# Pair one-hots of a group by one broadcast comparison, with the weights put on the place rows by GpSimd

## The chip, the cores and the metric

One core of a Trainium2 chip runs the whole program. The metric is the device time of one execution in microseconds (us). The kernel before took 2555.01 us in the median of three runs (2551.72 to 2556.26).

## What is computed

The reference is a graph network on 3125 nodes with 128 features and 103125 edges (`src`, `dst`, sorted by `dst`, and a type from 0 to 3 for each edge):

```python
deg = max(segment_sum(ones, dst), 1);  d = deg ** -0.5
h = relu(layernorm(x)); feat = h
for i in range(10):                                    # hops
    agg = segment_sum(feat[src] * (d[dst] * d[src])[:, None], dst)
    feat = (0.9 * agg + 0.1 * h) * reg[i] + (1 - reg[i]) * feat
x = x + feat
e = relu(layernorm(x))
for _ in range(4):                                     # gated steps
    m = (e @ W_msg.T + b_msg).reshape(n, 4, 128)
    e = gru_cell(segment_sum(m[src, edge_type], dst), e, ...)
return x + e
```

## The kernel before

The kernel never gathers rows. It first counts, for every pair of nodes, the edges between them, by type, as small digits packed in bytes (`big1`), and then does every segment sum as products with these counts. The stages are: setup (0 to 63 us of the profiled execution), counting (63 to 521 us), degrees and factors (to 559 us), ten hops (L691, L706), and four gated steps (L787 and others). The change is in the counting stage.

**The counting stage.** The nodes are cut into 125 groups of 25 targets (`Q = 125`). The edges lie in 825 chunks of 125, one edge per partition and one chunk per column of the tables `keys` (target and source folded into one number), `tab[:, 0]` (the place of the source, 0 to 124) and `tab[:, 1]` (the weight: a power of two that says type and lane). As the edges are sorted by target, a group's edges lie in a window of at most `W = 8` columns, but for rare extra ones (one in this data, L975 to L980 and L612).

For group `q` the engines do this:

- GpSimd (`stage`, L361 to L366): reads the window's first column, waits until the one-hots of two groups earlier have been made (`s_hot`), subtracts the group's offset from 8 keys into `win` (L364), and copies 8 weights (L365) and 8 places (L366). It signals `s_wst`.
- VectorE (`onehots`, L959 to L968): waits for `s_wst` and for TensorE to have used the buffer (`s_hot_used`). One comparison makes the place one-hots of all 8 columns, 128 x 8 16-bit elements (L964). Then 8 operations of 228 elements (`KP`) make the pair one-hots, one per column (L967): equal to the key, times the weight. Each signals `s_hot`.
- TensorE (`count`, L600 to L606): waits for a free bank (`s_taken`) and, before each of its 8 products, for that column's one-hots. Stationary operand: the 125 x 128 place one-hots of a column, read at a step of 8 elements (16 bytes). Moving operand: 228 pair columns. The 8 products add up in one of 8 banks of PSUM.
- ScalarE (`evacuate`, L456 to L461): writes the 228 sums as integers into `words`. After every 8 groups (a block) `part_lanes` (L463 to L472) parts the bytes into `packed` in three operations, and SyncE stores the block to DRAM (16 stores, L309).
- VectorE (`sum_digits`, L983 to L995): once per block, six operations on `packed` that sum the four types' digits into `big1`.

VectorE's order is written out by hand: 4 groups ahead, then blocks of 8 groups with a digit sum behind each, two blocks to an iteration of a loop of 7, then the rest; the last digit sum comes after the stage. One-hots are double buffered. The constants that the comparisons read (`iota_pair`, 228 elements, L346, and `iota_place`, 128 x 8, L348) are made by GpSimd in the setup; VectorE first waits for the constants at L910. Behind the stage TensorE sums the degrees (L647).

A second way through the kernel (`over_any > 0`, the "general" functions) is for inputs whose counts overflow the digits. It does not run here.

```python
def stage(n, q, b, hot, staged):
    pool.wait_ge(hot, W * n + W)
    pool.tensor_tensor(win[0:CH, b, 0, :], keys[0:CH, ds(lo, W)], ..., ALU.subtract)
    pool.tensor_copy(win[0:CH, b, 1, :], tab[0:CH, 1, ds(lo, W)])
    pool.tensor_copy(win_p[0:CH, b, :], tab[0:CH, 0, ds(lo, W)]).then_inc(staged, 1)
```

Of the kernel before, what the change touches and what calls it, by code (L numbers as in the profile page):

```python
# [51 lines left out]
KQ = 1024  # L52
# [5 lines left out]
BANKS = 8  # L58

# [22 lines left out]
def build(nc, x, src, dst, edge_type, layer_reg, w_msg, b_msg, w_ih, w_hh, b_ih, b_hh, out):  # L82
# [7 lines left out]
    with ctx:  # L90
# [68 lines left out]
        with ExitStack() as b:  # L159
            keys = sb("keys", [128, PAD], F32, b)  # L160
            tab = sb("tab", [128, 2, PAD], F16, b)
            win = sb("win", [128, 2, 2, W], F32, b)
            win_p = sb("win_p", [128, 2, W], F16, b)
            win_x = sb("win_x", [128, 3], F32, b)
            hot_pair = sb("hot_pair", [128, 2, W, KP], F16, b)
# [3 lines left out]
            iota_pair = sb("iota_pair", [128, KP], F16, b)  # L169
# [24 lines left out]
        with ExitStack() as b:  # L194
            words = sb("words", [128, 2, KP, BQ], I32, b)
            packed = sb("packed", [128, 2, BLOCK_BYTES], U8, b)
            dig = sb("dig", [128, 3, BLOCK_BYTES // 4], I32, b)
# [58 lines left out]
        s_wst, s_hot, s_hot_used = sem("window_staged"), sem("onehots_made"), sem("onehots_used")  # L256
# [80 lines left out]
        def _(pool):  # L337
# [8 lines left out]
            pool.iota(iota_pair[:, :], [[1, KP]], base=0, channel_multiplier=0,  # L346
# [35 lines left out]
            with pool.If(over_any > 0):  # L382
                pool.wait_ge(s_tables, 1)
                pool.iota(iota_pair_g[:, :], [[1, CA + 1]], base=0, channel_multiplier=0,
                          allow_small_or_imprecise_dtypes=True).then_inc(s_iota_g, 1)
                with pool.Fori(0, LOADS) as load:
# [26 lines left out]
        def _(act):  # L413
# [43 lines left out]
            def evacuate(blk, b, j):  # L457
                q = BQ * blk + j
                act.wait_ge(s_hot_used, W * q + 3 * W)
                summed(q, extras, s_more_used)  # L460
                act.activation(words[:, b, :, j], ps[:, j, 0:KP], ACT.Copy, scale=float(ONE)).then_inc(s_taken, 1)  # L461

            def part_lanes(blk, turn, b, last):  # L463
                act.wait_ge(s_taken, last + 1 + BANKS)
                act.wait_ge(s_digits, blk + 1)
                act.wait_ge(s_packed[b], 16 * turn + 16)
                lanes = words[:, b, :, :].bitcast(U8).rearrange("p n (q l) -> p (n q) l", l=4)
                for l in range(LANES):
                    n = min(LANE, TILES - l * LANE) * TILES * BQ
                    at = l * LANE * TILES * BQ  # L470
                    ins = act.activation(packed[:, b, at:at + n], lanes[:, 0:n, l], ACT.Copy)
                ins.then_inc(s_bytes, 1)  # L472

            def block_of(turn, b, n):
                blk = 2 * turn + b
                act.wait_ge(s_bytes, blk + 1)
                for j in range(n):
                    evacuate(blk, b, j)
                part_lanes(blk, turn, b, BQ * blk + n - 1)

            with act.Fori(0, NB // 2 - 1) as i:
                block_of(i, 0, BQ)
                block_of(i, 1, BQ)
            block_of(NB // 2 - 1, 0, BQ)
            block_of(NB // 2 - 1, 1, Q - (NB - 1) * BQ)
# [79 lines left out]
        def _(pe):  # L565
# [31 lines left out]
            pe.sem_inc(s_hot_used, 2 * W)  # L597
# [40 lines left out]
            with pe.Fori(0, NB - 1) as i:  # L638
                for j in range(BQ):
                    count(BQ * i + j, j % 2, j)  # L640
            for j in range(Q - (NB - 1) * BQ):
                count(BQ * (NB - 1) + j, j % 2, j)
# [194 lines left out]
        def _(dve):  # L837
# [30 lines left out]
            dve.memset(keys[:, :], -1e6)  # L868
# [73 lines left out]
            dve.sem_inc(s_hot, 2 * W)  # L942
# [16 lines left out]
            def onehots(q, b):  # L959
# [3 lines left out]
                dve.wait_ge(s_hot_used, W * q + W)  # L963
                TT(hot_place[0:CH, b, :, :], iota_place[0:CH, :, :],  # L964
                   win_p[0:CH, b:b + 1, :].broadcast_to([CH, 128, W]), ALU.is_equal)
                for w in range(W):
                    TS(hot_pair[0:CH, b, w, :], iota_pair[0:CH, :], win[0:CH, b, 0, w:w + 1],  # L967
                       win[0:CH, b, 1, w:w + 1], ALU.is_equal, ALU.mult).then_inc(s_hot, 1)  # L968
                with dve.If(many > 0):
                    lo = dve.value_load(windows[0:1, ds(q, 1)], min_val=0, max_val=NCH - 1)  # L970
                    with dve.Fori(0, many) as j:
# [8 lines left out]
                        TS(hot_pair_x[0:CH, :], iota_pair[0:CH, :], win_x[0:CH, 0:1], win_x[0:CH, 2:3],  # L980
                           ALU.is_equal, ALU.mult).then_inc(s_more, 1)

            def sum_digits(blk, b):  # L983

                dve.wait_ge(s_bytes, blk + 3)
                x, low, high, lower = packed[:, b, :].bitcast(I32), dig[:, 0, :], dig[:, 1, :], dig[:, 2, :]
                u16 = [d.bitcast(DT.uint16) for d in (low, high, lower)]
# [49 lines left out]
            for j in range(BQ):  # L1037
                onehots(BQ * (NB - 2) + HEAD + j, j % 2)
            sum_digits(NB - 2, 0)
            for q in range(BQ * (NB - 1) + HEAD, Q):  # L1040
                onehots(q, q % 2)
# [55 lines left out]
            with dve.If(over_any > 0):  # L1097
# [6 lines left out]
                step_g(TS(tab_e[width, 1, :], tab_e[width, 0, :], 3, None, ALU.logical_shift_right))  # L1104
                step_g(STT(out=keys[width, :], in0=tab_e[width, 1, :], scalar=float(LANE * TILES), in1=keys[width, :],
# [12 lines left out]
                dve.wait_ge(s_iota_g, 1)  # L1118
# [353 lines left out]
```

## Time and profile before

| | |
|---|---|
| median of three runs | 2555.01 us (2551.72 to 2556.26) |
| the profiled execution | 2550.86 us |
| its span | 2549.3 us |
| TensorE clock granted over the span | 0.921 of full |
| busy over the span: PE, PEld, DVE, ACT, POOL | 2190.8, 1440.7, 1488.7, 335.0, 134.9 us |
| counting stage | 63.01 to 521.21 us |

Engines in the rows: PE is a TensorE product, PEld the load of its stationary operand, DVE is VectorE, ACT is ScalarE, POOL is GpSimd, SP is SyncE. A name with q is the engine's sequencer. L605 is line 605 of the kernel. The clock column gives the granted TensorE clock as a share of 2.4 GHz. A group of instructions shows its busy time, the mean duration of one, and the time in which the engine stood idle just before them with what ended it. Durations overlap where a next instruction starts before the one in front has fully ended, so paces are read from starts. GpSimd's spans are rough.

### The profile page before, as it was taken

The page shows a single profiled execution, that of the slowest core. Times are in us where ns is not written, and L with a number is a line of the kernel's source. Part 1 is how long each engine was busy: PE and PEld are TensorE (multiplying, and loading weights), DVE is VectorE, ACT ScalarE, POOL GpSimd, SP SyncE. Part 2 cuts the span into 40 slices and gives each one's busy share as a digit, 9 for nine tenths or more (in the row PEclk, how much of TensorE's full clock was granted, in tenths as well). Part 3 has the DMA queues.
Part 4 walks back from the last instruction along what each step waited for, and adds up shares of the span by engine and source line. Part 5 has one row for each costly group of instructions (what it writes and reads, how often), then busy time and mean ns, then how long its engine had stood idle before and what let it go on. Part 6 is the DMA issues. An engine that isn't in the chain of part 4 may idle for free.

```text
span 2549.3 us, 41289 instructions
## 1 busy us (share of the span) xinstructions
PE 2190.8 (86%) x14375; PEld 1440.7 (57%) x14886; DVE 1488.7 (58%) x3473; ACT 335.0 (13%) x494; POOL 134.9 (5%) x391
## 2 busy tenths in 40 slices
PE   1544545559999999999799999999999999999996
PEld 1322333348999898988644455444554446544464
DVE  6988999977777777777662234522444324442243
ACT  0322223330000000000121011210112100220000
POOL 1322222200000000000000000000000000000000
PEclk9996555559999999999899999999999999999998
DMA  2000000010000000001400000000000000000001
GB/s 72 21 21 21 21 21 21 28 41 2 1 2 2 2 2 2 1 2 49 139 1 1 1 1 1 1 1 1 1 1 1 1 1 1 1 1 1 1 1 50
DMA packets 22188, 34.32 MB, mean 13 GB/s; under 512 B 2450, under 2 KB 18442, under 8 KB 21469
## 3 DMA queue, kind: packets, MB, share of 16 engines
q1 hardware_dynamic: 19025, 30.56, 3.5%
q8 instruction: 127, 2.08, 0.3%
q10 hardware_dynamic: 2944, 0.93, 0.2%
q14 instruction: 92, 0.75, 0.1%
HBM read 18.04 MB, written 13.45 MB: 12 GB/s over the span
## 4 chain that ended last, share of the span: by engine, by line
PE 75%; DVE 15%; issue 5%; DVEq 2%; DMA 2%; ACT 0%; POOLq 0%; ACTq 0%; POOL 0%
PE ps L787 41%; PE ps L706 26%; DVE hot_pair L967 8%; PE ps L739 3%; PE ps L727 2%; DVEq L961 2%; DVE dig L990 1%; DVE hot_place L964 1%; DVE big L993 1%; DMA big<-in_L_gnn_w_hh 1%; PE ps L647 1%; DMA x_after_hops<-x 1%; PE ps L691 1%; PE ps L605 1%; DVE dig L992 1%
## 5 line engine op out<-in xcount | busy, mean ns | idle before, releaser
L787 PE MATMUL ps<-slots,m_parts 125*128 125x500 fp8e4 (+1 forms) x5600 | 1088.0, 354 | 6.6 <-DVE m_parts L1337 5.2
L787 PEld LDWEIGHTS ps<-slots,m_parts 125*128 125x128 f16 x5600 | 547.4, 98 | 495.7 <-issue 10.0
L706 PE MATMUL ps<-parts,big 125*128 125x256 f16 x6125 | 669.6, 273 | 6.8 <-issue 4.2
L706 PEld LDWEIGHTS ps<-parts,big 125*128 125x128 fp8e4 x6125 | 591.3, 98 | 63.6
L605 PE MATMUL ps<-hot_pair,hot_place 125*128 125x228 f16 x1000 | 230.6, 400 | 256.5 <-DVE hot_pair L967 256.5
L1255 DVE TENSOR_SCALAR slots<-big 128x3200 int32<-128x3200 int32 (+1 forms) x112 | 244.1, 2183 | 279.8 <-PE ps L787 279.7
L605 PEld LDWEIGHTS ps<-hot_pair,hot_place 125*128 125x128 f16 x1000 | 143.1, 149 | 343.8 <-DVE hot_pair L967 283.1
L967 DVE TENSOR_SCALAR hot_pair<-iota_pair,win 125x228 f16<-125x228 f16 x1000 | 262.5, 334 | 3.1 <-issue 3.1
L1357 DVE SCALAR_TENSOR_TENSOR r_parts<-ps,over,r_parts 128x500 f16<-128x500 f32 (+1 forms) x28 | 19.1, 684 | 230.1 <-ACT r_parts L527 230.1
L1364 DVE SCALAR_TENSOR_TENSOR gate_r<-ps,over,gate_r 128x500 f32<-128x500 f32 (+1 forms) x28 | 19.1, 682 | 229.3 <-PE ps L739 221.8
L1183 DVE SCALAR_TENSOR_TENSOR hop_tmp<-ps,coef,g 125x128 f32<-125x128 f32 x250 | 87.6, 350 | 97.9 <-PE ps L706 94.4
L461 ACT ACTIVATE words<-ps 128x228 int32<-128x228 f32 x125 | 72.0, 602 | 354.4 <-PE ps L605 352.2
L964 DVE TENSOR_TENSOR hot_place<-iota_place,win_p 125x1024 f16<-125x1024 f16 x125 | 85.5, 684 | 48.2 <-issue 32.1
L727 PE MATMUL ps<-w_parts,emb_parts 128*125 128x512 f16 x300 | 84.7, 397 | 17.7 <-DVE m_full L1343 9.3
L527 ACT ACTIVATE r_parts<-ps,over 128x500 f16<-128x500 f32 (+1 forms) x28 | 17.7, 634 | 618.6 <-PE ps L787 618.6
L427 ACT ACTIVATE rs<-rs 125x25 f32<-125x25 f32 x3 | 0.7, 224 | 708.7 <-DVE rs L852 708.7
L1185 DVE SCALAR_TENSOR_TENSOR hop_tmp<-ps,coef,hop_tmp 125x128 f32<-125x128 f32 x250 | 87.8, 351 | 8.9
L1164 DVE TENSOR_SCALAR parts<-hop_tmp,scale 125x128 f16<-125x128 f32 x225 | 64.3, 286 | 36.4 <-DVE hop_tmp L1185 33.0
L1178 DVE SCALAR_TENSOR_TENSOR g<-hd,anchor,hop_tmp 125x128 f32<-125x128 f32 x225 | 79.0, 351 | 9.4 <-DVE hop_tmp L1177 0.7
L1167 DVE SCALAR_TENSOR_TENSOR parts<-hop_tmp,scale,parts 125x128 f16<-125x128 f32 x225 | 79.1, 352 | 8.0
L364 POOL TENSOR_TENSOR win<-keys,q_off 125x8 f32 (+1 forms) x125 | 65.3, 523 | 332.7 <-DVE hot_pair L967 318.5
L1343 DVE SCALAR_TENSOR_TENSOR m_full<-ps,bias_msg 125x512 f32<-125x512 f32 x100 | 68.3, 689 | 24.6 <-PE ps L727 23.6
(200 smaller groups left out, 1130.2 us busy)
## 6 DMA issues: line engine op xcount, KB each, us to landing
packed_counts<-packed SPq DMA_DIRECT2D x16, 625.0 KB, 3.3
big<-packed_counts SPq DMA_DIRECT2D x4, 1600.0 KB, 7.3
big<-packed_counts SPq DMA_DIRECT2D x3, 1200.0 KB, 6.5
hd<-in_x SPq DMA_DIRECT2D x1, 1562.5 KB
x_again<-in_x SPq DMA_DIRECT2D x1, 1562.5 KB
x_after_hops<-x SPq DMA_DIRECT2D x1, 1562.5 KB
big<-x_after_hops SPq DMA_DIRECT2D x1, 1562.5 KB
out<-big SPq DMA_DIRECT2D x4, 250.0 KB
```

The lines of the kernel that those rows point to most:

```text
L605: pe.matmul(ps[:, j, 0:KP], hot_place[0:CH, b, :, w], hot_pair[0:CH, b, w, :], start=w == 0, stop=w == W - 1, skip_group_check=True).then_ ...
L706: last = pe.matmul(ps[:, n % RING, 0:2 * F], tot_f8[0:Q, c, a, :], both((parts0, parts1)[par], a), start=a == 0, stop=a == TILES - 1)
L727: last = pe.matmul(ps[0:Q, 6 + a % 2, :], emb_parts[:, h, a, :], w_parts[:, w, :], start=n == 0, stop=n == 2)
L739: last = pe.matmul(out, g_parts[:, w, j * F:(j + 1) * F], value(h), start=start and m == 0, stop=stop and m == 2)
L787: last = pe.matmul(ps[:, k % 2, 0:SIZES[k] * Q], m_parts[0:Q, a, h, t * F:(t + 1) * F], slots_f8[0:Q, t % 2, 0:SIZES[k], a, 0:Q], start=a ...
L964: TT(hot_place[0:CH, b, :, :], iota_place[0:CH, :, :], win_p[0:CH, b:b + 1, :].broadcast_to([CH, 128, W]), ALU.is_equal)
L967: TS(hot_pair[0:CH, b, w, :], iota_pair[0:CH, :], win[0:CH, b, 0, w:w + 1], win[0:CH, b, 1, w:w + 1], ALU.is_equal, ALU.mult).then_inc(s_h ...
L1167: return STT(out=at[:, 1, :], in0=value, scalar=power, in1=at[:, 0, :], op0=ALU.mult, op1=ALU.subtract)
L1178: step(STT(out=tile_of(g, c), in0=tile_of(hd, c), scalar=anchor[0:Q, ds(h, 1)], in1=hop_tmp[0:Q, 2, :], op0=ALU.mult, op1=ALU.add))
L1183: step(STT(out=hop_tmp[0:Q, 0, :], in0=bank[:, 0:F], scalar=column(coef, c), in1=tile_of(g, c), op0=ALU.mult, op1=ALU.add))
L1185: step(STT(out=hop_tmp[0:Q, 1, :], in0=bank[:, F:2 * F], scalar=column(coef, c), in1=hop_tmp[0:Q, 0, :], op0=ALU.mult, op1=ALU.add))
L1255: TS(slots[:, t % 2, 0:n * 4].bitcast(I32).rearrange("p (n b w) -> p n b w", b=NB, w=2), big1[:, first:first + n * 4].bitcast(I32).rearran ...
```

## The change

The pair one-hots of a group are made by one comparison of 228 x 8 elements, laid out with the column innermost as the place one-hots are. They carry no weight now. The weights go onto the place one-hots: VectorE's place comparison writes `marks`, and GpSimd multiplies them by the 8 weights into `weighed` in one operation of 1024 elements. TensorE waits once per group for both and reads `weighed` as stationary and `hot_pair` at a step of 8 elements as moving operand. Buffers become four deep (`DEPTH`). GpSimd stages group q+2 (two operations, now into 16-bit tiles) ahead of multiplying group q. To keep the keys exact in 16 bits the offset per group is 456 instead of 1024. ScalarE evacuates two groups later and lays its three lane operations between the evacuations of the next block. The digit sum has five operations: the nibble fold is a multiplication by 1 + 1/16 on 16-bit numbers and one mask. VectorE goes 8 groups ahead instead of 4, and places the digit sum before the last one-hots of a block.

```diff
+KQ = 456
+DEPTH = 4
@@ GpSimd
-            pool.iota(iota_pair[:, :], [[1, KP]], base=0, channel_multiplier=0,
+            pool.iota(iota_pair[:, :, :], [[1, KP], [0, W]], base=0, channel_multiplier=0,
...
-            with pool.Fori(0, Q // 2) as i:
-                stage(2 * i, 2 * i, 0, s_hot, s_wst)
-                stage(2 * i + 1, 2 * i + 1, 1, s_hot, s_wst)
-            stage(Q - 1, Q - 1, 0, s_hot, s_wst)
+            def stage_window(q, b):
+                lo = pool.value_load(windows[0:1, ds(q, 1)], min_val=0, max_val=NCH)
+                pool.wait_ge(s_hot_used, q + 1)
+                pool.tensor_copy(win_pw[0:CH, b, :, :], tab[0:CH, :, ds(lo, W)])
+                pool.tensor_tensor(win_key[0:CH, b, :], keys[0:CH, ds(lo, W)], q_off[0:CH, ds(q, 1)].broadcast_to([CH, W]),
+                                   ALU.subtract).then_inc(s_wst, 1)
+            def weigh(q, b):
+                pool.wait_ge(s_marks, q + 1)
+                pool.tensor_tensor(weighed[0:CH, b, :, :], marks[0:CH, b, :, :],
+                                   win_pw[0:CH, b, 1:2, :].broadcast_to([CH, 128, W]), ALU.mult).then_inc(s_weighed, 1)
+            stage_window(0, 0)
+            stage_window(1, 1)
+            with pool.Fori(0, (Q - 3) // DEPTH) as i:
+                for j in range(DEPTH):
+                    stage_window(DEPTH * i + j + 2, (j + 2) % DEPTH)
+                    weigh(DEPTH * i + j, j)
@@ ScalarE
-                act.wait_ge(s_hot_used, W * q + 3 * W)
+                act.wait_ge(s_hot_used, q + 1 + DEPTH)
...
+            def block_of(turn, b, n, turn_before):
+                for j in range(n):
+                    if j >= 2:
+                        evacuate(blk, b, j - 2)
+                    elif turn_before is not None:
+                        evacuate(2 * turn_before + 1 - b, 1 - b, BQ - 2 + j)
+                    if 3 <= j < 3 + LANES and turn_before is not None:
+                        part_lane(turn_before, 1 - b, j - 3, 16 * turn_before + BQ * (1 - b) + BQ - 1)
@@ TensorE
                 pe.wait_ge(s_taken, q + 1)
+                pe.wait_ge(s_pairs, q + 1)
+                pe.wait_ge(s_weighed, q + 1)
                 for w in range(W):
-                    pe.wait_ge(s_hot, W * q + w + 2 * W + 1)
-                    pe.matmul(ps[:, j, 0:KP], hot_place[0:CH, b, :, w], hot_pair[0:CH, b, w, :],
-                              start=w == 0, stop=w == W - 1, skip_group_check=True).then_inc(s_hot_used, 1)
+                    last = pe.matmul(ps[:, j, 0:KP], weighed[0:CH, b, :, w], hot_pair[0:CH, b, :, w],
+                                     start=w == 0, stop=w == W - 1, skip_group_check=True)
+                last.then_inc(s_hot_used, 1)
@@ VectorE
-                dve.wait_ge(s_hot_used, W * q + W)
-                TT(hot_place[0:CH, b, :, :], iota_place[0:CH, :, :],
-                   win_p[0:CH, b:b + 1, :].broadcast_to([CH, 128, W]), ALU.is_equal)
-                for w in range(W):
-                    TS(hot_pair[0:CH, b, w, :], iota_pair[0:CH, :], win[0:CH, b, 0, w:w + 1],
-                       win[0:CH, b, 1, w:w + 1], ALU.is_equal, ALU.mult).then_inc(s_hot, 1)
+                dve.wait_ge(s_hot_used, q + 1)
+                TT(marks[0:CH, b, :, :], iota_place[0:CH, :, :],
+                   win_pw[0:CH, b, 0:1, :].broadcast_to([CH, 128, W]), ALU.is_equal).then_inc(s_marks, 1)
+                TT(hot_pair[0:CH, b, :, :], iota_pair[0:CH, :, :],
+                   win_key[0:CH, b:b + 1, :].broadcast_to([CH, KP, W]), ALU.is_equal).then_inc(s_pairs, 1)
...
-                step(TT(u16[0], u16[0], u16[1], ALU.add))
-                TS(high, low, NIBBLES, None, ALU.bitwise_and)
-                step(TS(lower, low, 4, NIBBLES, ALU.logical_shift_right, ALU.bitwise_and))
-                step(TT(big1[:, :].bitcast(DT.uint16).rearrange("p (n q) -> p n q", q=64)[:, :, ds(4 * blk, 4)],
-                        u16[1].rearrange("p (n q) -> p n q", q=4), u16[2].rearrange("p (n q) -> p n q", q=4), ALU.add))
+                step(TT(low16, low16, high16, ALU.add))
+                step(TS(high16, low16, 1.0 + 1.0 / 16, None, ALU.mult))
+                step(TS(big1[:, :].bitcast(I32).rearrange("p (n q) -> p n q", q=32)[:, :, ds(2 * blk, 2)],
+                        high.rearrange("p (n q) -> p n q", q=2), NIBBLES, None, ALU.bitwise_and))
...
-            HEAD = BQ // 2
-            for j in range(HEAD):
-                onehots(j, j % 2)
+            for j in range(BQ):
+                onehots(j, j % DEPTH)
...
-                        onehots(2 * BQ * i + BQ * b + HEAD + j, j % 2)
-                    sum_digits(2 * i + b, b)
+                        onehots(2 * BQ * i + BQ * (b + 1) + j, j % DEPTH)
+                        if j == BQ - 2:
+                            sum_digits(2 * i + b, b)
```

## Rows read from the trace of the kernel before

**Rows 1.** The page's costliest groups of instructions: TensorE's count products and VectorE's pair one-hots.

```profile
L605 PE MATMUL ps<-hot_pair,hot_place 125*128 125x228 f16 x1000 | 230.6, 400 | 256.5 <-DVE hot_pair L967 256.5
...
L967 DVE TENSOR_SCALAR hot_pair<-iota_pair,win 125x228 f16<-125x228 f16 x1000 | 262.5, 334 | 3.1 <-issue 3.1
```

**Rows 2.** Busy time of each engine in the counting stage, then granted clock and DMA.

```profile
62.00:522.00 460.00, 230.94 (x1001) 143.19 (x1001) 419.10 (x1224) 138.47 (x169) 128.56 (x375) 0.67 0.05 22
```

**Rows 3.** Groups of instructions by line, from 60 to 525 us.

```profile
L964 DVE TENSOR_TENSOR hot_place<-iota_place,win_p 125x1024 f16<-125x1024 f16 x125 | 85.5, 684 | 48.2 <-issue 32.1 <-POOL win_p L366 15.2 <-DVE big L993 0.8
L461 ACT ACTIVATE words<-ps 128x228 int32<-128x228 f32 x125 | 72.0, 602 | 354.4 <-PE ps L605 352.2 <-PE ps L612 2.2
L471 ACT ACTIVATE packed<-words 128x1800 uint8<-128x1800 uint8 (+1 forms) x47 | 71.8, 1589 | 1.1
...
L990 DVE TENSOR_TENSOR dig<-dig 128x2500 uint16<-128x2500 uint16 x15 | 22.0, 1468 | 0.5
```

**Rows 4.** Timeline of the stage's start: start, duration (us), engine, line, operation.

```profile
63.01 0.19 POOL L364 TENSOR_TENSOR win<-keys,q_off 125x8 f32 x1 [14.17 <-issue]
63.17 0.18 POOL L365 CAST win<-tab 125x8 f32 x1
...
63.46 0.19 POOL L364 TENSOR_TENSOR win<-keys,q_off 125x8 f32 x1
63.52 0.69 DVE L964 TENSOR_TENSOR hot_place<-iota_place,win_p 125x1024 f16<-125x1024 f16 x1 [15.20 <-POOL win_p L366]
63.60 0.67 POOL L365 CAST win<-tab 125x8 f32 x1
64.13 2.09 DVE L967 TENSOR_SCALAR hot_pair<-iota_pair,win 125x228 f16<-125x228 f16 x8
...
66.14 0.68 DVE L964 TENSOR_TENSOR hot_place<-iota_place,win_p 125x1024 f16<-125x1024 f16 x1
```

**Rows 5.** Timeline of one digit sum.

```profile
154.94 0.80 DVE L988 TENSOR_SCALAR dig<-packed 128x1250 int32<-128x1250 int32 x1
155.20 1.32 POOL L364 TENSOR_TENSOR win<-keys,q_off 125x8 f32 x1 [1.75 <-DVE hot_pair L967]
155.66 0.80 DVE L989 TENSOR_SCALAR dig<-packed 128x1250 int32<-128x1250 int32 x1
...
156.49 1.47 DVE L990 TENSOR_TENSOR dig<-dig 128x2500 uint16<-128x2500 uint16 x1
...
156.59 1.41 POOL L366 COPY win_p<-tab 125x8 f16 x1
158.00 0.81 DVE L991 TENSOR_SCALAR dig<-dig 128x1250 int32<-128x1250 int32 x1
...
159.68 1.46 DVE L993 TENSOR_TENSOR big<-dig 128x2500 uint16 x1
```

**Rows 6.** Timeline of the setup: two of GpSimd's constants, and VectorE's first use.

```profile
12.94 0.84 POOL L342 IOTA chunk<- 128x825 f32 x1
...
14.11 1.93 POOL L348 IOTA iota_place<- 128x1024 f16 x1
...
38.66 0.37 DVE L910 TENSOR_SCALAR q<-q 128x1 f32<-128x1 f32 x1
```

**Rows 7.** Loads of stationary operands (source view: min/median/max), and the granted clock beside them.

```profile
L605 PEld LDWEIGHTS ps<-hot_pair,hot_place x96: 142/145/169, 64.5 to 95.3; 125*128 125x128 f16 x96
...
64.00:90.00 26.00, 17.92 (x80) 11.45 (x80) 26.00 (x91) 8.35 (x11) 7.48 (x30) 1.00 0.01 2
...
L612 PEld LDWEIGHTS ps<-hot_pair_x,hot_place_x 125*128 125x128 f16 x1 | 0.1, 103 | 0.8 <-DVE hot_pair_x L980 0.8
...
559.80 0.15 PEld L570 LDWEIGHTS <-ones 128*128 128x128 f16 x1
...
556.00:565.00 9.00, 6.03 (x30) 4.61 (x37) 8.59 (x26) 7.34 (x25) 0.45 (x1) 0.51 0.33 126
```

**Rows 8.** Timeline: the stage's last pair one-hots.

```profile
519.13 2.08 DVE L967 TENSOR_SCALAR hot_pair<-iota_pair,win 125x228 f16<-125x228 f16 x8
```

More of the change, by code:

```diff
@@ L51 @@
 KP = 228
-KQ = 1024
+KQ = 456
+KG = 1024
+NOWHERE = -4096.0
 BQ = 8
@@ L196, in build @@
             packed = sb("packed", [128, 2, BLOCK_BYTES], U8, b)
-            dig = sb("dig", [128, 3, BLOCK_BYTES // 4], I32, b)
+            dig = sb("dig", [128, 2, BLOCK_BYTES // 4], I32, b)
+            hot_pair = sb("hot_pair", [128, DEPTH, KP, W], F16, b)
+            marks = sb("marks", [128, DEPTH, 128, W], F16, b)
+            weighed = sb("weighed", [128, DEPTH, 128, W], F16, b)
         with ExitStack() as b:
@@ L366, in stage @@
                 pool.tensor_copy(win_p[0:CH, b, :], tab[0:CH, 0, ds(lo, W)]).then_inc(staged, 1)
-            with pool.Fori(0, Q // 2) as i:
-                stage(2 * i, 2 * i, 0, s_hot, s_wst)
-                stage(2 * i + 1, 2 * i + 1, 1, s_hot, s_wst)
-            stage(Q - 1, Q - 1, 0, s_hot, s_wst)
+            def stage_window(q, b):
[14 more added lines that the diff above has]
+                    weigh(DEPTH * i + j, j)
+            for q in range((Q - 3) // DEPTH * DEPTH, Q):
+                if q + 2 < Q:
+                    stage_window(q + 2, (q + 2) % DEPTH)
+                weigh(q, q % DEPTH)
             def share_largest():
@@ L458, in evacuate @@
                 q = BQ * blk + j
-                act.wait_ge(s_hot_used, W * q + 3 * W)
+                act.wait_ge(s_hot_used, q + 1 + DEPTH)
                 summed(q, extras, s_more_used)
+                if j == 0:
+                    act.wait_ge(s_bytes, blk + 1)
                 act.activation(words[:, b, :, j], ps[:, j, 0:KP], ACT.Copy, scale=float(ONE)).then_inc(s_taken, 1)
[L463 to L466, printed above, removed]
-                lanes = words[:, b, :, :].bitcast(U8).rearrange("p n (q l) -> p (n q) l", l=4)
[L468 to L472, printed above, removed]
@@ L474, in block_of, with part_lane @@
-            def block_of(turn, b, n):
+            def part_lane(turn, b, l, last):
+                blk = 2 * turn + b
+                if l == 0:
+                    act.wait_ge(s_taken, last + 1 + BANKS)
+                    act.wait_ge(s_digits, blk + 1)
+                    act.wait_ge(s_packed[b], 16 * turn + 16)
+                lanes = words[:, b, :, :].bitcast(U8).rearrange("p n (q l) -> p (n q) l", l=4)
+                n = min(LANE, TILES - l * LANE) * TILES * BQ
+                at = l * LANE * TILES * BQ
+                ins = act.activation(packed[:, b, at:at + n], lanes[:, 0:n, l], ACT.Copy)
+                if l == LANES - 1:
+                    ins.then_inc(s_bytes, 1)
@@ L486, in _ @@
+            block_of(0, 0, BQ, None)
+            with act.Fori(0, NB // 2 - 1) as i:
+                block_of(i, 1, BQ, i)
+                block_of(i + 1, 0, BQ, i)
+            block_of(NB // 2 - 1, 1, Q - (NB - 1) * BQ, NB // 2 - 1)
+            evacuate(NB - 1, 1, 3)
+            part_lane(NB // 2 - 1, 0, 2, BQ * (NB - 1) - 1)
+            evacuate(NB - 1, 1, 4)
+            for l in range(LANES):
+                part_lane(NB // 2 - 1, 1, l, Q - 1)
             root(1)
@@ L639, in _ @@
                 for j in range(BQ):
-                    count(BQ * i + j, j % 2, j)
+                    count(BQ * i + j, j % DEPTH, j)
             for j in range(Q - (NB - 1) * BQ):
-                count(BQ * (NB - 1) + j, j % 2, j)
+                count(BQ * (NB - 1) + j, j % DEPTH, j)
             pe.wait_ge(s_digits, NB + 2)
@@ L1033, in _ @@
                     for j in range(BQ):
-                        onehots(2 * BQ * i + BQ * b + HEAD + j, j % 2)
-                    sum_digits(2 * i + b, b)
+                        onehots(2 * BQ * i + BQ * (b + 1) + j, j % DEPTH)
+                        if j == BQ - 2:
+                            sum_digits(2 * i + b, b)
             steps.done(NB // 2 - 1)
-            for j in range(BQ):
-                onehots(BQ * (NB - 2) + HEAD + j, j % 2)
+            for q in range(BQ * (NB - 1), Q):
+                onehots(q, q % DEPTH)
             sum_digits(NB - 2, 0)
-            for q in range(BQ * (NB - 1) + HEAD, Q):
-                onehots(q, q % 2)
             dve.wait_ge(s_wout, 1)
@@ L1104, in _ @@
                 step_g(TS(tab_e[width, 1, :], tab_e[width, 0, :], 3, None, ALU.logical_shift_right))
+                step_g(TS(tab_f[width, :], keys[width, :], 1.0 / KQ, MAGIC, ALU.mult, ALU.add))
+                step_g(TS(tab_f[width, :], tab_f[width, :], -MAGIC, None, ALU.add))
+                step_g(STT(out=keys[width, :], in0=tab_f[width, :], scalar=float(KG - KQ), in1=keys[width, :],
+                           op0=ALU.mult, op1=ALU.add))
                 step_g(STT(out=keys[width, :], in0=tab_e[width, 1, :], scalar=float(LANE * TILES), in1=keys[width, :],
```

31 lines of the change are left out of this document (14 added, 17 removed).

## The prediction, made before the changed kernel was run

> **What bounds the kernel now.** I read the page's costliest groups first, then the engines' busy time over the counting stage, then that stage's groups, and last single groups in the timeline.
>
> The change touches only the stage in which the pair counts are made. It runs from the first staged window to the end of the last pair one-hots, 63.01 to 521.21 us [rows 4, 8]: 458.2 us, 3.67 us for each of the 125 groups. The profiled execution took 2550.86 us, 4 us under the median of the three runs (2555.01), so I make the sum against the former and add 4 us at the end. No later stage is edited.
>
> In the stage VectorE is busy 419 of 460 us, TensorE 231, ScalarE 138, GpSimd 129 [rows 2]. TensorE's waits before its products are for one producer, the pair one-hots [rows 1]. So VectorE sets the pace. A group costs it one place comparison (start to next start 0.61 us) and eight pair operations (262 ns apart); from one place comparison to the next are 2.62 us [rows 1, 4]. A digit sum, from the first operation's start to the last one's end, is 6.20 us [rows 5], 15 of them in the stage, 0.74 us per group. The rest is 32 us of issue gaps in 14 places [rows 3], 0.26 per group. 2.62 + 0.74 + 0.26 = 3.62, against 3.67.
>
> The rows to look at twice are GpSimd's. Its subtraction of 8 elements takes 0.19 us when nothing is in the way [rows 4], yet the one begun at 155.20 during a VectorE digit operation lasts 1.32 us, to 156.52, just past the end at 156.46 of the second of two such operations. The copy of 8 elements begun at 156.59 lasts 1.41 us, to 158.00: the VectorE operation of two inputs begun at 156.49 ends at 157.96 [rows 5]. The cast begun at 63.60 lasts 0.67 us, to 64.27, and the place comparison beside it ends at 64.21 [rows 4]. **GpSimd stands still while VectorE runs an operation of this kind.** Before, that cost nothing, as GpSimd had almost nothing to do.
>
> **The change, part by part.**
>
> VectorE, pairs: eight operations of 262 ns (2.10 us) go; one comparison of 1824 elements with two inputs comes. The place comparison is the same form with 1024 elements, 684 ns [rows 3]; the digit operation with two 16-bit inputs and 2500 elements takes 1468 ns [rows 3]. Slope (1468 - 684) / 1476 = 0.53 ns per element, so 684 + 800 x 0.53 = 1.11 us, and the next one starts some 0.08 us before the end, as it does behind the place comparison: 1.03 us. The place comparison stays. VectorE's own need per group falls from 2.71 to 1.64 us.
>
> VectorE, digits: six operations become five. The two masks on packed bytes and the first addition stay: 0.72 + 0.83 + 1.51 from start to next start [rows 5]. A 16-bit operation with a constant is new: 2500 elements, between 0.80 us (what the masks of 1250 words take [rows 5]) and 2.6 us (twice the slope above, 1.06 ns per element). I take 0.80. The last mask, 0.81, writes into the counts. 4.7 us instead of 6.2, so 0.56 per group.
>
> GpSimd: staging goes from three small operations to two, 0.16 us apart [rows 4], 0.31 per group. The multiplication of 1024 comes in. No row has a long GpSimd operation with two inputs. The nearest are its constants: 1024 16-bit elements in the same 128 by 8 form, 1.93 us; 825 of 32 bits, 0.84 us [rows 6]. Low end: 1.02 ns per element, 1.04 us. High end: the 1.93 plus one more stream at 1.02 ns, 2.97 us. I take 1.93, for its count, type and form. The Trainium skill (GPSIMD Engine Reference, Performance versus the Vector engine) gives 4497 ns for a two-input operation of 2048 fp32 elements; an estimate by it is 2.2 us, which would put 34 us on the sum. No row here shows such an operation.
>
> How the two add: VectorE's comparisons of group q+2 and GpSimd's multiplication of group q are released by the same event, the staging of q+2. If they exclude each other, a group takes 0.61 + 1.03 + 1.93 + 0.31 = 3.88 us. Each hand-over adds the 0.05 us by which GpSimd's ends lag VectorE's [rows 4, 5], two of them: 3.98. Times 125 is 498 us. The 15 digit sums exclude it as well: 70 us. The issue gaps (2.3 us each) now lie beside the multiplication, all but 14 x 0.4 = 5 us. Sum 573 us, against 458: **+115 us**.
>
> The Trainium skill (SBUF — State Buffer, Who interferes with whom) says that a VectorE operation with two SBUF inputs and a GpSimd operation that reads SBUF exclude each other for the whole instruction, whichever comes first. By this rule the sum is the 573 us, and rival A below, 150 us under the time of before, is ruled out. The trace agrees for a GpSimd that comes second (0.67, 1.32 and 1.41 us); no row has VectorE waiting for GpSimd.
>
> TensorE: still eight products of 228 columns per group, the moving operand now read at a step of 16 bytes. The stationary operand has that step already: its load takes 145 ns at the full granted clock, a dense one 103, and a dense one 150 at half clock [rows 7]. So the step costs 42 ns in 128 columns at 2.4 GHz and nothing at 1.2. For 228 columns that is at most 95 + 75 = 170 ns at full and 190 at half clock, 1.5 us per group. Hidden under 3.98, and it would be under 2.45. If the step doubled the time at half clock, 3.0 us: still hidden in my forecast, not in the first rival.
>
> ScalarE: 72.0 us of evacuations and 71.8 of lane parting [rows 3], 1.15 us per group in either order; the new order only interleaves them. Hidden; if that cover went, TensorE would have eight banks of slack. The queue of SyncE issues the same 16 stores.
>
> Constants: the pair ramp grows from 228 to 1824 elements, 1.7 to 3.4 us on GpSimd. The place ramp ends at 16.04 us and VectorE first waits for all constants at 38.66 [rows 6]: hidden. Behind the stage the granted clock is half [rows 7], and I take it to stay so: 0, at best a few us of gain. The general path is not run. The last digit sum, behind the stage, gives 1.5 us back.
>
> Sum: 2551 + 115 - 1.5 + 4 = **2668 us**. With the multiplication at 1.3 or 2.97 us it is 2590 or 2798.
>
> **The rivals.**
>
> A. GpSimd comes first and both run side by side. For it: GpSimd's subtraction begun at 63.46 ended in its usual 0.19 us although the place comparison began at 63.52, and that comparison took 0.69 us, as always [rows 4]. In the new order GpSimd reaches the multiplication at about the moment its staging releases VectorE, so it would mostly be first. Against: those were 8 elements, over before the comparison had read much. GpSimd's period is 1.93 + 0.31 = 2.24 us and some register work; VectorE's is 1.64 + 0.56 + 0.26 = 2.46. So 2.46 x 125 = 308 us, 150 less: 2403. At 2.97 us GpSimd bounds at 3.3: 2510; TensorE at 3.0 us: 2475. This is the case on the other side; what decides it is whether a long GpSimd read holds VectorE back.
>
> B. They exclude each other, but the multiplication runs near 1.04 us. Then a group takes 0.61 + 1.03 + 1.04 + 0.31 + 0.10 = 3.09, times 125 is 386, with digits and gaps 461: 2556, no difference. 1.04 us is the point at which the exclusion costs nothing net. For: the 32-bit ramp. Against: the 16-bit one of the same form, and two inputs.
>
> C. The one-hot comparison doesn't pack two elements per cycle (its second input is a repeated row of 8). Against: the place comparison has the same pattern and does. Without it the pairs cost 0.53 x 1824 = 1.0 us more per group, under exclusion 120 us more. 2 in 100.
>
> **How the numbers follow.** What can be told from no change here is about 0.2%, 5 us. Exclusion with a multiplication above 1.1 us: 0.57, with 2590 to 2750 as its own range. A, with its partial forms: 0.32. B: 0.09, split 0.03 faster, 0.04 same, 0.02 slower. C: 0.02, slower. So faster 0.35, same 0.04, slower 0.61. The range must reach both signs: from 2405, which holds nearly all of A, to 2750, which leaves out the slowest multiplications and C.
>
> **What would show it.** Right: the multiplication's own time near 2 us; 4 us from one place comparison to the next; VectorE idle before the place or pair comparison, released by GpSimd or stretched while it runs; GpSimd busy share of the stage over 90%; TensorE waiting for the multiplication, not for the pairs. Wrong: pairs and multiplication overlapping at full length, a stage of 300 to 350 us. It would also be wrong if products of 228 columns followed one another at over 300 ns, or if a digit sum came out over 6 us.

## The result, and the profile after

The changed kernel took 2617.94 us (median of four runs, 2615.95 to 2619.85) against 2554.86 before: ratio 1.0252, 95% interval 1.0239 to 1.0266. It is **slower by 63 us**. Its profiled execution has a span of 2616.4 us, 67.1 more than before.

The page's costliest groups of the changed kernel (columns as in [rows 1]); they answer to [rows 1] and to the first of [rows 3]:

```profile
L647 PE MATMUL ps<-hot_pair,weighed 125*128 125x228 f16 x1000 | 426.7, 587 | 128.7 <-POOL weighed L385 126.2
...
L385 POOL TENSOR_TENSOR weighed<-marks,win_pw 125x1024 f16<-125x1024 f16 x125 | 273.7, 2190 | 63.1 <-DVE marks L1006 63.1
L1006 DVE TENSOR_TENSOR marks<-iota_place,win_pw 125x1024 f16<-125x1024 f16 x125 | 208.6, 1669 | 47.5 <-POOL win_key L380 29.1
L1008 DVE TENSOR_TENSOR hot_pair<-iota_pair,win_key 125x1824 f16<-125x1824 f16 x125 | 162.5, 1300 | 0.0
```

Three things stand here. The place comparison, the same operation as before, went from 684 to 1669 ns in the mean. TensorE's 1000 products went from 230.6 to 426.7 us of busy time. And the producer that TensorE waits for is now GpSimd, not VectorE.

Busy time by engine over the counting stage (columns as in [rows 2]):

```profile
62.00:588.00 526.00, 426.36 (x1001) 135.51 (x1001) 469.91 (x325) 136.72 (x169) 435.37 (x374) 1.00 0.04 18
```

VectorE has fewer instructions (325 for 1224) and more busy time. Much of that is waiting inside an instruction. The timeline of VectorE over two groups and the start of a digit sum shows it:

```profile
137.64 2.37 DVE L1006 TENSOR_TENSOR marks<-iota_place,win_pw 125x1024 f16<-125x1024 f16 x1
139.93 1.10 DVE L1008 TENSOR_TENSOR hot_pair<-iota_pair,win_key 125x1824 f16<-125x1824 f16 x1
141.12 2.37 DVE L1006 TENSOR_TENSOR marks<-iota_place,win_pw 125x1024 f16<-125x1024 f16 x1
143.41 1.09 DVE L1008 TENSOR_TENSOR hot_pair<-iota_pair,win_key 125x1824 f16<-125x1824 f16 x1
145.57 1.51 DVE L1029 TENSOR_SCALAR dig<-packed 128x1250 int32<-128x1250 int32 x1 [1.07 <-ACT packed L503]
147.00 0.80 DVE L1030 TENSOR_SCALAR dig<-packed 128x1250 int32<-128x1250 int32 x1
147.84 3.19 DVE L1031 TENSOR_TENSOR dig<-dig 128x2500 uint16<-128x2500 uint16 x1
151.06 0.84 DVE L1032 TENSOR_SCALAR dig<-dig 128x2500 uint16<-128x2500 uint16 x1
152.06 1.46 DVE L1033 TENSOR_SCALAR big<-dig 128x1250 int32 x1 [0.16 <-DVE dig L1032]
```

And GpSimd beside it:

```profile
137.57 1.89 POOL L385 TENSOR_TENSOR weighed<-marks,win_pw 125x1024 f16<-125x1024 f16 x1
139.72 0.35 POOL L379 COPY win_pw<-tab 125x16 f16 x1 [0.26 <-PE ps L647]
140.02 1.06 POOL L380 TENSOR_TENSOR win_key<-keys,q_off 125x8 f16 x1
141.05 1.89 POOL L385 TENSOR_TENSOR weighed<-marks,win_pw 125x1024 f16<-125x1024 f16 x1
```

GpSimd's multiplication starts at 137.57, 0.07 us ahead of the place comparison, and ends at 139.46. The comparison needs 0.68 us alone and takes 2.37, to 140.01. Then the pair comparison runs (139.93 to 141.03), and GpSimd's subtraction of 8 elements begun at 140.02 ends only at 141.08. A period is 141.12 - 137.64 = 3.48 us, just under the sum of the three long operations, 0.61 + 1.03 + 1.89 = 3.53. In the digit sum the addition of two 16-bit inputs takes 3.19 us instead of 1.46. (These rows are typical: the medians are 2362 ns for the place comparison and 1096 for the pairs. Their means, 1669 and 1300, mix them with groups in which the multiplication meets the pair comparison, which then takes up to 2796 ns.)

The stage's end (TensorE, then VectorE):

```profile
575.14 13.43 PE L647 MATMUL ps<-hot_pair,weighed 125*128 125x228 f16 x32 [0.90 <-POOL weighed L385]
```

```profile
578.94 2.80 DVE L1008 TENSOR_TENSOR hot_pair<-iota_pair,win_key 125x1824 f16<-125x1824 f16 x1
587.74 0.81 DVE L1029 TENSOR_SCALAR dig<-packed 128x1250 int32<-128x1250 int32 x1 [6.00 <-ACT packed L503]
```

Here TensorE runs 32 products without a pause: (13.43 - 0.59) / 31 = **0.41 us each**, 3.3 us per group. VectorE is done at 581.74, TensorE not before 588.57. The digit sum begun at 587.74 is one more than the kernel before has behind its last one-hots: there 15 of the 16 lie in the stage, here 14, as VectorE now goes 8 groups ahead.

**Where the 67 us of the profiled executions came from.** From the first staging to the last pair one-hots: 458.2 us before, 519.6 after, +61.4. From there to the degree sums: 13.0 before (521.21 to 534.25), 24.0 after (581.74 to 605.73), +11.0. From the degree sums to the first hop: +3.3, not explained. The start: -0.8. Behind the first hop's start: -7.7, which is +2.7 in the hops and -10.4 in the gated steps; the latter goes with the granted clock (last section). With rounding the sum is 67.2.

### The profile page after: what moved, and what is told of

Its sections match the earlier page's. It is cut to its first block, busy times and chain, and to the rows that moved or that the text cites. A ratio compares the mean times of both kernels' runs of the same rounds, so it can differ in the third digit from the quotient of the medians.

```text
span 2616.4 us, 39261 instructions
## 1 busy us (share of the span) xinstructions
PE 2384.9 (91%) x14375; PEld 1433.2 (55%) x14886; DVE 1546.7 (59%) x2582; ACT 333.3 (13%) x494; POOL 445.5 (17%) x391
## 4 chain that ended last, share of the span: by engine, by line
PE 83%; POOL 5%; issue 5%; DVE 4%; DMA 1%; POOLq 1%; ACT 0%; DVEq 0%; ACTq 0%
PE ps L830 40%; PE ps L749 25%; PE ps L647 11%; POOL weighed L385 3%; PE ps L782 3%; PE ps L770 2%; POOL win_pw L379 1%; POOLq L377 1%; DMA x_after_hops<-x 1%; PE ps L690 1%; PE ps L734 1%; POOL win_key L380 1%; DVE slots L1297 0%; DVE m_full L1385 0%; DVE tab L947 0%
## 5 line engine op out<-in xcount | busy, mean ns | idle before, releaser
L647 PE MATMUL ps<-hot_pair,weighed 125*128 125x228 f16 x1000 | 426.7, 587 | 128.7 <-POOL weighed L385 126.2
L647 PEld LDWEIGHTS ps<-hot_pair,weighed 125*128 125x128 f16 x1000 | 135.4, 148 | 419.2 <-issue 419.2
L385 POOL TENSOR_TENSOR weighed<-marks,win_pw 125x1024 f16<-125x1024 f16 x125 | 273.7, 2190 | 63.1 <-DVE marks L1006 63.1
L1006 DVE TENSOR_TENSOR marks<-iota_place,win_pw 125x1024 f16<-125x1024 f16 x125 | 208.6, 1669 | 47.5 <-POOL win_key L380 29.1
L1008 DVE TENSOR_TENSOR hot_pair<-iota_pair,win_key 125x1824 f16<-125x1824 f16 x125 | 162.5, 1300 | 0.0
L380 POOL TENSOR_TENSOR win_key<-keys,q_off 125x8 f16 (+1 forms) x125 | 102.6, 821 | 7.5 <-issue 7.5
```

The costliest lines, as they stand in the source:

```text
L380: pool.tensor_tensor(win_key[0:CH, b, :], keys[0:CH, ds(lo, W)], q_off[0:CH, ds(q, 1)].broadcast_to([CH, W]), ALU.subtract).then_inc(s_wst, 1)
L385: pool.tensor_tensor(weighed[0:CH, b, :, :], marks[0:CH, b, :, :], win_pw[0:CH, b, 1:2, :].broadcast_to([CH, 128, W]), ALU.mult).then_inc( ...
L647: last = pe.matmul(ps[:, j, 0:KP], weighed[0:CH, b, :, w], hot_pair[0:CH, b, :, w], start=w == 0, stop=w == W - 1, skip_group_check=True)
L1006: TT(marks[0:CH, b, :, :], iota_place[0:CH, :, :], win_pw[0:CH, b, 0:1, :].broadcast_to([CH, 128, W]), ALU.is_equal).then_inc(s_marks, 1)
L1008: TT(hot_pair[0:CH, b, :, :], iota_pair[0:CH, :, :], win_key[0:CH, b:b + 1, :].broadcast_to([CH, KP, W]), ALU.is_equal).then_inc(s_pairs, 1)
```

## The experiments

How far the pieces of the change that have no run of their own (four buffers, VectorE's longer lead, ScalarE's order) help or harm is not shown. Two theories of the changed kernel. **X**: VectorE's comparisons and GpSimd's multiplication exclude each other, and their sum of 3.5 us per group is the pace. **P**: TensorE's products, 3.3 us per group since their moving operand is read at a step of 16 bytes, are the pace. Either could give a stage of about 520 us. All runs were compared with the kernel before on the same chip (2555.24 us beside the first four, 2555.54 beside the last four).

**No multiplication.** GpSimd only stages the windows. The counts carry no weights, and the overflow flag is held at 0.

```diff
-                weigh(q, q % DEPTH)
...
-                pe.wait_ge(s_weighed, q + 1)
+                pe.wait_ge(s_marks, q + 1)
...
-                pe.matmul(ps[:, j, 0:KP], weighed[0:CH, b, :, w], ...
+                pe.matmul(ps[:, j, 0:KP], marks[0:CH, b, :, w], ...
```

> Leaves out the multiplication by the weights (TensorE reads the unweighted place one-hots, and the overflow flag is held at 0), all else as in the changed kernel. Theory X (exclusion of VectorE's comparisons and GpSimd's multiplication sets the pace, 0.61 + 1.03 + 1.89 = 3.53 us per group, products are second with 8 x 0.41 = 3.28): the comparisons take 0.68 and 1.10 us throughout, the pace falls only to the products' 3.28, a stage of 410 to 425 us instead of 526, 2500 to 2520 us. Theory P (the products at a 16-byte step set the pace and the exclusion is hidden): TensorE's 427 us busy plus its present waits stay, 2590 to 2618.

Measured: 2524.40 us (ratio 0.9884, 0.9867 to 0.9900). That is 94 us off the changed kernel, and rules out P. It is 4 us above the range that X gave. The groups of the stage:

```profile
L641 PE MATMUL ps<-hot_pair,marks 125*128 125x228 f16 x1000 | 412.2, 589 | 50.2 <-DVE hot_pair L1002 50.2
...
L1002 DVE TENSOR_TENSOR hot_pair<-iota_pair,win_key 125x1824 f16<-125x1824 f16 x125 | 137.5, 1100 | 0.0
L1000 DVE TENSOR_TENSOR marks<-iota_place,win_pw 125x1024 f16<-125x1024 f16 x125 | 86.0, 688 | 100.0 <-POOL win_key L380 70.2 <-issue 22.5 <-DVE big L1027 6.0
```

Both comparisons are back at their own length (1100 and 688 ns), and TensorE, busy for 412 of the 438 us from 62 to 500 us, is now the main bound. It is not the only one: it waits 50 us for VectorE, and VectorE's digit sums wait 59 us for ScalarE, which follows TensorE.

**A step of 4 bytes, multiplication kept.** The pair one-hots are laid out as 4 blocks of 228 x 2. The comparison is still one operation of 1824.

```diff
-            hot_pair = sb("hot_pair", [128, DEPTH, KP, W], F16, b)
+            hot_pair = sb("hot_pair", [128, DEPTH, W // 2, KP, 2], F16, b)
...
-                ... hot_pair[0:CH, b, :, w],
+                ... hot_pair[0:CH, b, w // 2, :, w % 2],
```

> The pair one-hots laid out as 4 blocks of 228 x 2, so that TensorE's moving operand has a step of 4 bytes instead of 16; GpSimd's multiplication stays, the result is complete. X: one product every 0.10 to 0.11 us at full clock or 0.19 at half, TensorE busy falls to under 250 us, but the pace stays at 3.5 us per group and the time only falls by the tail behind the stage, the digit sums' share of backlog and the like: 2590 to 2612. P: the stage falls with the products, to about 2.5 to 3 us per group, 2450 to 2530.

Measured: 2610.80 us (1.0222, 1.0205 to 1.0239). TensorE's busy time is halved and the time falls by 7 us:

```profile
L385 POOL TENSOR_TENSOR weighed<-marks,win_pw 125x1024 f16<-125x1024 f16 x125 | 297.6, 2381 | 52.0 <-DVE marks L1006 52.0
L647 PE MATMUL ps<-hot_pair,weighed 125*128 125x228 f16 x1000 | 213.6, 390 | 334.4 <-POOL weighed L385 332.6 <-ACT words L492 1.8
L1006 DVE TENSOR_TENSOR marks<-iota_place,win_pw 125x1024 f16<-125x1024 f16 x125 | 208.6, 1668 | 47.6 <-POOL win_key L380 29.4 <-issue 9.1 <-DVE big L1035 5.0
```

The place comparison still takes 1668 ns, and TensorE waits 333 us for the multiplication. X holds: the price of the products is real but hidden, except at the stage's end.

**Both.**

> Both: no multiplication and a step of 4 bytes (weights left out, flag held at 0). X and P alike: VectorE sets the pace at 1.64 us per group + 0.56 for the digit sums + 0.26 for gaps = 2.46, stage 308 us, 2395 to 2420. If it stays near the first of these runs (2500 to 2520), neither the step nor the exclusion was what held the products, and something else (waits, banks, ScalarE) does.

Measured: 2408.69 us (0.9434, 0.9418 to 0.9450), in the range expected. The four kernels make a square: with the multiplication 2618 (16 bytes) and 2611 (4 bytes), without it 2524 and 2409. The step costs 7 us under the exclusion and 116 us without it.

**The multiplication on VectorE, step of 4 bytes.** The result is complete, and GpSimd only stages the windows.

```diff
-                weigh(q, q % DEPTH)
...
+                dve.wait_ge(s_marks, q + 1)
+                TT(weighed[0:CH, b, :, :], marks[0:CH, b, :, :],
+                   win_pw[0:CH, b, 1:2, :].broadcast_to([CH, 128, W]), ALU.mult).then_inc(s_weighed, 1)
```

> Complete result: the multiplication of 1024 is done by VectorE behind the pair comparison, step of 4 bytes. X: 0.61 + 1.03 + 0.61 = 2.25 us per group, + 0.56 + 0.26 = 3.07, stage 384 us, 2470 to 2490: faster than both kernels. P, or any theory in which GpSimd's work is free: slower than the run with GpSimd's multiplication and the same step.

Measured: **2486.25 us** (0.9736, 0.9720 to 0.9752). It is faster than both kernels: 69 us under before, 132 under the changed one. VectorE's three operations in the stage:

```profile
L1002 DVE TENSOR_TENSOR hot_pair<-iota_pair,win_key 125x1824 f16<-125x1824 f16 x125 | 137.4, 1099 | 0.0
L1000 DVE TENSOR_TENSOR marks<-iota_place,win_pw 125x1024 f16<-125x1024 f16 x125 | 85.4, 683 | 50.5 <-POOL win_key L380 32.4 <-issue 12.7 <-DVE big L1032 5.0
L1007 DVE TENSOR_TENSOR weighed<-marks,win_pw 125x1024 f16<-125x1024 f16 x125 | 85.0, 680 | 0.0
```

The multiplication that cost GpSimd 1.89 us costs VectorE 0.68, and since the two engines did not run these operations side by side, moving it to GpSimd was moving it to the slower one on one shared path.

**The multiplication on VectorE, step of 16 bytes.** The same, with the changed kernel's layout.

> Complete result: VectorE does the multiplication, but the pair one-hots keep the changed kernel's layout, so TensorE reads its moving operand at a step of 16 bytes. Theory X (a product at this step costs 0.41 us, hidden behind the exclusion in the changed kernel and bare without it): 8 x 0.41 = 3.28 us per group against VectorE's 3.1, so 2515 to 2535, as in the run without a multiplication (2524). Rival (what held that run was something of its missing multiplication or of the queue's order): 2480 to 2492, as with a step of 4 bytes.

Measured: 2543.60 us (0.9958, 0.9944 to 0.9972). This rules out the rival. It lies 9 us over X's range. VectorE's 3.1 and TensorE's 3.3 us per group are near each other, and each waits for the other: TensorE is busy 412.3 us of the stage and idle for 69.9 before its products, for VectorE, and VectorE's digit sums wait 42.7 us for ScalarE, which follows TensorE. So of the 69 us of the better kernel 57 hang on the layout.

**A step of 8 bytes**, 2 blocks of 228 x 4.

> As the run with VectorE's multiplication and a step of 4 bytes (2486), but 2 blocks of 228 x 4, a step of 8 bytes. If the cost comes from how many columns of one partition share a 16-byte line (8 columns dense, 4 at 4 bytes, 2 at 8, 1 at 16) and two suffice: products as fast as at 4 bytes, 2480 to 2492. If it grows in proportion to the step: about 0.25 to 0.3 us a product, 2.0 to 2.4 us per group, still under VectorE's 3.1, so the same time; the spacing of the products in a group tells (0.19 or less against 0.25 to 0.3).

Measured: 2491.29 us (0.9745, 0.9729 to 0.9761), inside what both forecasts gave. The spacing of the products tells more, in eight products that follow one another. The rows are of this run (8 bytes), of the run with GpSimd's multiplication and a step of 4 bytes, of the last run below (dense columns), and of the run without a multiplication at 4 bytes:

```profile
214.69 1.83 PE L641 MATMUL ps<-hot_pair,weighed 125*128 125x228 f16 x8 [0.38 <-DVE weighed L1007]
```

```profile
300.57 1.71 PE L647 MATMUL ps<-hot_pair,weighed 125*128 125x228 f16 x8 [2.21 <-POOL weighed L385]
```

```profile
301.50 1.72 PE L647 MATMUL ps<-hot_pair,weighed 125*128 125x228 f16 x8 [2.14 <-DVE hot_pair L1009]
```

```profile
254.44 1.04 PE L641 MATMUL ps<-hot_pair,marks 125*128 125x228 f16 x8 [0.57 <-DVE hot_pair L1002]
```

Less the last product's own length (0.387, 0.393, 0.396 and 0.272 us) and over 7: 0.21 us at 8 bytes, 0.19 at 4, 0.19 dense, and 0.11 at 4 bytes in the last row. The clock column reads 1.00 beside all four, yet the last row runs at another pace than the rest. Here are the lengths (least, median and most) of the last row's run as a whole and of L605 before, between 350 and 500 us:

```profile
L641 PE MATMUL ps<-hot_pair,marks x1000: 261/272/393, 64.3 to 376.2; 125*128 125x228 f16 x167
```

```profile
L605 PE MATMUL ps<-hot_pair,hot_place x322: 396/396/418, 349.6 to 499.9; 125*128 125x228 f16 x161
```

The last row's products have the length of the hops' at a granted clock of 1.00 (273 ns); those of the other three have the length that the kernel before shows at a granted clock of 0.50 (the second view). So only the first three can be compared, and 0.11 must not be set against 0.21. At this pace a step of 4 bytes costs nothing, one of 8 bytes a tenth, and one of 16 bytes (0.41 us) about as much again as the product itself. That is near the first case (two columns in 16 bytes suffice), not the proportional one. No run shows 8 bytes at the pace of the last row, and no row tells at which pace the products at 16 bytes ran.

**The old digit sum** in the kernel with VectorE's multiplication and a step of 4 bytes.

> As the run with VectorE's multiplication and a step of 4 bytes (2486), but with the digit sum of six operations of the kernel before. Without GpSimd in the way the two sums take 6.20 and 5.5 us from first start to last end (the last mask of the new one takes 1.46 us, not 0.81): 16 x 0.7 = 11 us more, 2492 to 2502. If the new form's worth is what was predicted (1.5 us each): 2505 to 2515. If the digit sum is hidden: no difference.

Measured: 2504.31 us (0.9798, 0.9782 to 0.9815), 18 us more, between the two forecasts. Within the sums only 11 to 12 us can be seen: 6.22 against 5.50 us in the mean from the first start to the last end, 16 times. From one digit sum to the next the kernels differ by 1.03 us in the mean of 14. Where the other 0.3 us per block goes is open, as are some 2 us behind the first hop's start.

**Pairs column by column.** The changed kernel, but with eight one-input comparisons per group and dense columns.

```diff
-                TT(hot_pair[0:CH, b, :, :], iota_pair[0:CH, :, :],
-                   win_key[0:CH, b:b + 1, :].broadcast_to([CH, KP, W]), ALU.is_equal).then_inc(s_pairs, 1)
+                for w in range(W):     # win: keys, now 32-bit
+                    last = TS(hot_pair[0:CH, b, w, :], iota_pair[0:CH, :, 0], win[0:CH, b, 0, w:w + 1], None, ALU.is_equal)
+                last.then_inc(s_pairs, 1)
```

> The changed kernel with GpSimd's multiplication, but the pair one-hots made by eight one-input comparisons of 228 dense columns, without weights (0.26 us each); TensorE's moving operand is dense. Complete result. VectorE alone: 0.61 + 2.10 + 0.69 + 0.26 = 3.7 us per group. If one-input comparisons from SBUF exclude GpSimd's reads as the two-input ones do: 0.61 + 2.10 + 1.89 + 0.7 = 5.3, 2720 to 2780. If they leave GpSimd free: VectorE's pace with only the place comparison waiting at times, 3.7 to 4.2, 2555 to 2630.

Measured: 2672.98 us (1.0457, 1.0440 to 1.0475), in neither range. The expectation was wrong in a term: without the factor these comparisons are about 0.2 us apart, not 0.26. The source view of that line, and the timeline of GpSimd's and VectorE's operations in one group, settle the question all the same:

```profile
L1009 DVE TENSOR_SCALAR hot_pair<-iota_pair,win x1000: 264/270/2014, 63.4 to 642.4; 125x228 f16<-125x228 f16 x167
```

```profile
301.92 3.33 DVE L1009 TENSOR_SCALAR hot_pair<-iota_pair,win 125x228 f16<-125x228 f16 x8
302.08 1.96 POOL L385 TENSOR_TENSOR weighed<-marks,win_pw 125x1024 f16<-125x1024 f16 x1 [1.50 <-DVE marks L1006]
...
305.18 0.68 DVE L1006 TENSOR_TENSOR marks<-iota_place,win_pw 125x1024 f16<-125x1024 f16 x1
```

Mostly 0.27 us, and up to 2.01 for one that meets the multiplication (1.96). Eight take 3.26 us, 1.66 more than 8 x 0.2. So these one-input comparisons exclude GpSimd's reads as well, though the period of 3.86 us is 0.23 under the sum, 0.60 + 1.6 + 1.89 = 4.09. [rows 5] had a case of it: the masks L988 and L989, beside which GpSimd's subtraction took 1.32 us, have one input. Whether the comparison with the factor (0.26 us apart) does so too, no run tells.

## Why the prediction was right, and where it was off

The direction and the mechanism were right; the size was put at +115 us and measured at +63. The range (2405 to 2750) was made to hold rival A's faster kernel as well, so that 2618 lies in it says little; it also lies in the 2590 to 2750 of the main case alone. By the steps of the prediction:

- **VectorE sets the pace before** [rows 1, 2]: nothing contradicts it. In the run in which VectorE's own work set the pace of the new order (no multiplication, 4 bytes), the time was 2409; I had put that case at 2403.
- **Pairs, 1.11 us, next start at 1.03**: measured 1.10 (median 1.096) and 1.02 in runs without the multiplication. Right.
- **The multiplication, 1.93 us** [rows 6]: 1.89 to 1.96 when not held. The row of the same shape was the right one to take. The estimate by the Trainium skill (GPSIMD Engine Reference), 2.2 us, was 0.3 us too high here.
- **Exclusion**: shown. GpSimd did come first, by 0.07 us, as rival A had it, but VectorE then stood still: 2.37 us for 0.68. The rule of the Trainium skill (SBUF — State Buffer, Who interferes with whom) agrees with these rows in both directions. The rows of before could only show one, as GpSimd's operations were 8 elements long; rival A rested on exactly that gap. One of the three rows that I gave for the rule is no case of it: beside the 1.32 us of [rows 5] VectorE ran operations of one input.
- **The term that was mis-sized: staging and hand-overs, 0.31 + 0.10 us per group**. The period is 3.48 us, 0.05 under the three long operations alone. GpSimd's copy and subtraction run beside the two comparisons, and the subtraction ends with the pair comparison, so they cost nothing of their own. I had added operations of 8 elements at full length to a sum of times in which the path is held, though [rows 5] show that they hold nothing. The period came out 0.5 us under 3.98, 62 us in 125 groups and more than the whole difference; 0.41 of it is this term, 0.04 the shorter multiplication.
- **Digits and gaps, 75 us**: 519.6 - 125 x 3.48 = 85 us, and with 14 digit sums in the stage, not 15. The five operations take 5.5 us alone, not 4.7, mainly since the last mask, with its scattered output, takes 1.46 and not 0.81. They are stretched where they meet GpSimd (7.95 us from first start to last end), and each of the 14 waits about 1 us for ScalarE.
- **TensorE, at most 190 ns per product**: wrong, by more than a factor of two (410 ns). I took the step's price from a load of the stationary operand, 145 against 103 ns, as measured at full clock [rows 7]. That reading was wrong too. The load of 103 ns stands alone at 455.5 us, where the granted clock is 0.50, and the products of L605 take 396 ns both between 64 and 100 us (clock column 1.00) and between 350 and 500 us (0.50). At the slow pace the dense loads of the first hop take 150 to 151 ns. So the rows of before priced the step for neither operand. It was luck that the products stayed hidden, by 0.2 us per group, and the stage still came out near its sum.
- **The part behind the stage, -1.5 us**: it was +11.0. VectorE is through with the one-hots at 581.74. Its next digit sum waits 6.00 us for ScalarE, which waits for TensorE's backlog, and takes 5.4 us itself; before, this sum lay in the stage.
- **ScalarE's new order, nothing**: VectorE's digit sums waited 20.3 us in all for ScalarE (15 waits). With the same order and multiplication but a step of 4 bytes it was one wait of 3.3 us. So the waits came from the products' lateness, not from the order.
- **The clock**: I took it to stay at half behind the stage. In the changed kernel the clock column reads 1.00 all through the stage and into the hops, but that does not tell the pace. The first hop's products (least, median and most), and the busy times with the column around them:

```profile
L734 PE MATMUL ps<-parts,big x125: 272/273/421, 633.8 to 649.2; 125*128 125x256 f16 x125
```

```profile
600.00:700.00 100.00, 82.78 (x1211) 75.47 (x1256) 69.93 (x220) 15.16 (x52) 0.42 (x1) 1.00 0.05 19
```

The 421 ns are those of the first 16 products, up to 637 us; from 638 us on it is 273. Before, the first 24 products of that hop take 421 ns too, with 0.52 in the column. So TensorE came out of the stage at half pace in both, and a 1.00 ahead of the column's first change is no measure. The 625 degree products took 16.8 us in both. Of the four runs of the changed kernel the one with the lowest mean clock in its column, 0.875, was the quickest (2615.95 us).
- **The signs that I named**: the multiplication near 2 us, VectorE stretched beside it and TensorE waiting for it (126 us) all came. The period was to be 4 us and was 3.48; GpSimd's busy share was to be over 90% and was 83% (435 of 526 us). Two signs of being wrong came as well, products over 300 ns apart (410) and a digit sum over 6 us (7.95). Neither touched the exclusion; they are the terms above.
- **Rival A's sums**: with GpSimd at 3.28 us the sum is 2505, not 2510, and with TensorE at 3.0 us it is 2470, not 2475. It changes nothing.

In terms of the sum: +115 for the stage became +61, -1.5 for the part behind became +11, and the rest of the profiled executions differs by -5. The medians differ by 4 us less than the profiled executions, since only the one before lay 4 us under its median.

## What to carry to other kernels

Before work is moved from VectorE to GpSimd, add up the lengths of the operations of both that read SBUF, the on-chip memory in which these tiles lie: here they ran one after the other, so the work has to be cheaper on GpSimd, not merely parallel, and it was 1.89 us there against 0.68. When a layout is changed so that one engine can do its work in one operation, price what the other reader of that tile pays for the new step, and keep several of its columns within 16 bytes: blocks of 228 x 2 cost VectorE nothing, and TensorE's products followed one another as they did with dense columns (0.19 us in both). And in a sum over an exclusive path, count the time for which it is held, not the time that an instruction shows while it waits.

## What was not expected of the hardware

- Products of 228 columns of 16 bits follow one another every 0.41 us at a step of 16 bytes in the moving operand. At 8 bytes it is 0.21, at 4 bytes and dense 0.19, all three at half pace by the length of the products; at 4 bytes and full pace it is 0.11.
- The clock column of a trace can read 1.00 for hundreds of us while the products' lengths are those of half pace: 393 ns at 4 bytes between 300 and 480 us in the run with that step and GpSimd's multiplication, as between 520 and 580 us, where the column says 0.50 (390). The length and the spacing of products tell the pace, the column alone does not.
- A one-input comparison of 228 elements (0.27 us) takes up to 2.01 us when it meets a long GpSimd operation that reads.
- A last operation that writes 2 words out of every 32 takes 1.46 us for 1250 words, where a mask of as many words with a dense output takes 0.80.
- From the last hop product's start to the end the kernel before takes 1297.6 us, the changed kernel 1287.2 and the other runs 1288.1 to 1290.2. The granted clock goes with it: at 1571, 1891 and 2211 us the kernel before has 30 us at 0.89, and the changed kernel has 1.00 in the matching stretches (1649, 1969 and 2289 us). An estimate from this is 0.11 x 90 = 10 us, of the 10.4 that differ. Why the clock fell there in the one and not in the other, no run tried.
